# Cross attention and mixture of experts on one core: products twelve blocks behind the scores, splits and sums placed anew

## The reference

```python
def xattn(q, k, v, gamma):           # q = layernorm(x); k = v = ctx
    qk = einsum('bhdq,bhdl->bhql', qh, kh) / sqrt(dq)
    sm = softmax(qk, axis=-1)
    ret = einsum('bhql,bhdl->bhdq', sm, vh)
    return gamma * ret
x = x + xattn(layernorm(x), ctx, ctx, gamma)
def ffn(x, U, V, W1, b1, W2, b2):
    h = relu(x @ W1 + b1)
    alpha = softmax(h @ W2 + b2)     # 8 experts
    vx = einsum('krd,bsd->bskr', V, x)
    return einsum('bsk,bskd->bsd', alpha, einsum('kdr,bskr->bskd', U, vx))
x = x + ffn(layernorm(x), ...)
```

## Time and profile before

| | |
|---|---|
| three runs | 1687.66 us median (1683.01 to 1691.62) |
| the profiled execution | 1685.4 us, its span 1683.6 us |
| TensorE | 1568.5 us busy, 93% |
| VectorE | 993.7 us, 59% |
| ScalarE | 765.0 us, 45% |
| GpSimd | 715.3 us, 42% |
| DMA queue 1 | 56.3% of 16 engines' span, 293.84 MB |

### The profile page before, as it was taken

One profiled execution on the slowest core, in us unless ns is written; L12 is line 12 of the kernel. 1 busy time (PEld: TensorE's weight loads), 2 busy tenths in 40 slices (PEclk: granted clock), 3 DMA queues, 4 the chain that ended last, 5 costly groups with the idle time before them and its releaser, 6 DMA issues.

```text
span 1683.6 us, 21711 instructions
## 1 busy us (share of the span) xinstructions
PE 1568.5 (93%) x6496; PEld 1159.5 (69%) x6496; DVE 993.7 (59%) x1290; ACT 765.0 (45%) x1222; POOL 715.3 (42%) x523
## 2 busy tenths in 40 slices
PE   5989999898999989999967999999999999999999
PEld 3666666666666666666645787877878787787877
DVE  7888888888888888888754432433323242332312
ACT  5776766767676676767653312112121211212120
POOL 3887878888788887878751000000000000000000
PEclk9999999999999999999987999999999999999999
DMA  6989989999899888998886031120302112030302
GB/s 176 283 270 287 264 285 273 275 286 267 285 262 290 281 268 284 264 294 277 240 265 220 20 101 50 63 87 6 130 13 100 50 62 87 10 133 6 100 1 75
DMA packets 119963, 294.18 MB, mean 175 GB/s; under 512 B 26240, under 2 KB 31360, under 8 KB 119936
## 3 DMA queue, kind: packets, MB, share of 16 engines
q1 hardware_dynamic: 119936, 293.84, 56.3%
HBM read 125.87 MB, written 33.69 MB: 95 GB/s over the span
## 4 chain that ended last, share of the span: by engine, by line
PE 49%; POOL 26%; issue 15%; DMA 4%; SPq 3%; DVE 2%; ACT 1%; POOLq 0%; ACTq 0%; DVEq 0%
PE scores L928 21%; POOL pt_lo L342 15%; PE scores L971 11%; PE attended L989 10%; POOL k_lo L325 4%; POOL x_out L351 3%; PE spare L1008 2%; DMA x_res<-in_x 2%; SPq L223 2%; POOL v_lo L329 2%; PE scores L517 1%; PE scores L946 1%; PE scores L943 1%; DMA pt<-pb 1%; PE attended L539 1%
## 5 line engine op out<-in xcount | busy, mean ns | idle before, releaser
L342 POOL TENSOR_TENSOR pt_lo<-pt,pt_hi 128x512 fp32r<-128x512 f32 (+1 forms) x256 | 399.7, 1562 | 156.5 <-ACT pt_hi L411 156.5
L571 DVE TENSOR_REDUCE neg_max<-scores 128x1 f32<-128x1024 f32 x256 | 312.6, 1221 | 105.8 <-PE scores L517 105.5
L418 ACT ACTIVATE probs<-scores,neg_max 128x1024 f32<-128x1024 f32 x256 | 284.2, 1110 | 198.8 <-DVE neg_max L571 198.5
L580 DVE STREAM_TRANSPOSE pb<-probs 128x1024 f32<-128x1024 f32 x256 | 316.2, 1235 | 16.8 <-DMA pt<-pb 16.5
L853 POOL TENSOR_TENSOR rstd<-var_eps,minus_half 128x1 f32<-128x1 f32 x28 | 17.2, 613 | 609.6 <-DVE var_eps L1054 609.6
L517 PE MATMUL scores<-k_hi,q_hi 128*128 128x512 f32 x512 | 237.1, 544 | 20.5 <-ACT probs L418 11.3
L539 PE MATMUL attended<-pt_hi,v_hi 128*128 128x512 f32 x320 | 140.9, 440 | 88.4 <-POOL pt_lo L342 87.6
L411 ACT ACTIVATE pt_hi<-pt 128x512 fp32r<-128x512 f32 (+1 forms) x256 | 186.7, 729 | 63.8 <-DMA pt<-pb 59.2
L872 ACT ACTIVATE hidden<-scores,b_col 128x512 f32<-128x512 f32 x64 | 44.2, 690 | 351.3 <-PE scores L928 351.3
L928 PE MATMUL scores<-nt_hi,w_hi 128*128 128x512 f32 x512 | 200.9, 392 | 2.5 <-DVE w_lo L1079 2.5
L928 PE MATMUL scores<-nt_lo,w_hi 128*128 128x512 f32 x512 | 200.2, 391 | 0.0
(11 more groups left out here) (95 smaller groups left out, 2640.9 us busy)
## 6 DMA issues: line engine op xcount, KB each, us to landing
pt<-pb SPq DMA_DIRECT2D x512, 256.0 KB, 4.6
x_raw<-in_x SPq DMA_DIRECT2D x32, 512.0 KB, 6.3
k_raw<-in_ctx SPq DMA_DIRECT2D x32, 512.0 KB, 5.2
gain_row<-gains SPq DMA_DIRECT2D x64, 256.0 KB, 4.8
x_res<-in_x SPq DMA_DIRECT2D x32, 512.0 KB, 5.6
x<-x_out SPq DMA_DIRECT2D x64, 256.0 KB, 4.1
first_n<-x SPq DMA_DIRECT2D x32, 512.0 KB, 3.6
result<-x SPq DMA_DIRECT2D x64, 256.0 KB, 3.7
```

The lines of the kernel that those rows point to most:

```text
L342: nc.gpsimd.tensor_tensor(pt_lo[2 * parity + half][:, :, keys, :], pt[2 * parity + half][:, :, keys, :], as_f32(hi[half][q][:]), ALU.subtr ...
L418: nc.scalar.activation(probs[j % 2][:], scores[j % 2][:], ACT.Exp, bias=neg_max[:, j:j + 1], accum_out=row_sum[b][:, j:j + 1]).then_inc(s_ ...
L571: nc.vector.tensor_reduce(neg_max[:, j:j + 1], scores[j % 2][:], AX_X, ALU.max, negate=True).then_inc(s_max, 1)
L580: nc.vector.transpose(pb[half][:, :, j % HALF, :], probs[j % 2][:]).then_inc(s_blocks, 1)
```

## The change

The distance from scores to products becomes 12 blocks, for the low parts 10, for the high parts 9. The pieces of work beside them move to other blocks of the head. SP's queue gets another order: `load_v` fetches the values of the head that runs (before: of the next one) and stands behind the gather of the previous head's second half; each `spread_gain` stands a few issues behind its own `send_gain` and ahead of the next gather. Heads 1 to 3 are written out.

```diff
-    LAG = 10
+    LAG = 12
+    LOW_LAG = 10
+    HIGH_LAG = 9
@@ over_heads
-        slot(1, JB, 1, False, False)
-        with eng.Fori(1, heads // 2 - 1) as pair:
+        for h in range(1, 4):
+            slot(h, h * JB, h % 2, False, False)
+        with eng.Fori(2, heads // 2 - 1) as pair:
@@ sync, slot
             if not first:
                 gather(h - 1, n - JB, 1, 1 - parity)
+                sp.wait_ge(s_vlo, h)
+                load_v(h)
                 send_gain(h - 1, 0)
...
                 load_k(h + 2)
+            if not first:
+                spread_gain(h - 1, 0)
             if not (known and h < 2):
                 sp.wait_ge(s_pv, n - JB)
             load_v_native(h, parity)
-            if not last:
-                sp.wait_ge(s_vlo, h + 1)
-                load_v(h + 1)
-            if not first:
-                spread_gain(h - 1, 0)
+            if more:
+                sp.wait_ge(s_q32, h + 2)
+                load_x(h + 2)
+            gather(h, n, 0, parity)
             if not first:
                 send_gain(h - 1, 1)
...
                 load_residual(h - 1)
-            if more:
-                sp.wait_ge(s_q32, h + 2)
-                load_x(h + 2)
-            gather(h, n, 0, parity)
-            if not first:
                 spread_gain(h - 1, 1)
@@ gpsimd, slot
-                low_probs(quarter_in(h, n, j, parity, LAG - 1))
-                if j == 1 and not last:
+                low_probs(quarter_in(h, n, j, parity, LOW_LAG))
+                if j == 1 and not early:
+                    add_residual(h - 2, 0)
+                if j == 2 and not last:
                     low_keys(h + 1, 1 - parity)
-                if j == 3:
+                if j == 3 and not last:
+                    scale_of_queries(h + 1, 1 - parity)
+                if j == 5 and not early:
+                    add_residual(h - 2, 1)
+                if j == 6 and not last:
+                    low_queries(h + 1, 1 - parity)
+                if j == 7:
                     low_values(h, parity)
...
@@ scalar, slot
-                if j == 0 and not first:
+                if j == 1 and not first:
                     gains(h - 1, 0)
-                if j == 4 and not first:
+                if j == 5 and not first:
                     gains(h - 1, 1)
-                high_probs(quarter_in(h, n, j, parity, LAG - 2))
-                if j == 0 and not last:
+                high_probs(quarter_in(h, n, j, parity, HIGH_LAG))
+                if j == 1 and not last:
                     high_keys(h + 1, n + JB, 1 - parity)
-                if j == 2:
+                if j == 4:
                     high_values(h, n, parity)
-                if j == 3 and not last:
+                if j == 4 and not last:
                     queries(h + 1, 1 - parity)
@@ vector, slot
+                if j in (0, 4) and not early:
+                    scale_attended(h - 2, n - 2 * JB, j // 4)
+                if j in (0, 4) and not first:
+                    inverse_sums(h - 1, j // 4, 1 - parity)
+                if j in (1, 2) and not last:
+                    statistics(h + 1, 1 - parity, j - 1)
+                if j == 3 and not last:
                     variance(h + 1, 1 - parity)
...
```

More of the change, by code:

```diff
@@ L364, in slot @@
             for j in range(JB):
-                low_probs(quarter_in(h, n, j, parity, LAG - 1))
-                if j == 1 and not last:
+                low_probs(quarter_in(h, n, j, parity, LOW_LAG))
+                if j == 1 and not early:
+                    add_residual(h - 2, 0)
+                if j == 2 and not last:
                     low_keys(h + 1, 1 - parity)
-                if j == 3:
-                    low_values(h, parity)
[L370 to L377, removed]
+                if j == 3 and not last:
[5 more added lines that the diff above has]
+                if j == 7:
+                    low_values(h, parity)
                 if last and j in (4, 6):
@@ L390, in gpsimd @@
         for j in range(JB):
-            low_probs(quarter_in(h, n, j, 0, LAG - 1))
+            low_probs(quarter_in(h, n, j, 0, LOW_LAG))
+            if j == 1:
+                add_residual(h - 2, 0)
             if j in (1, 2):
                 first_factor(j + 1)
-            if j == 3:
+            if j == 5:
                 add_residual(h - 2, 1)
-            if j == 7:
-                add_residual(h - 1, 0)
-        low_probs(quarter_in(h + 1, n + JB, 0, 1, LAG - 1))
+        for j in range(2):
+            low_probs(quarter_in(h + 1, n + JB, j, 1, LOW_LAG))
+        add_residual(h - 1, 0)
         add_residual(h - 1, 1)
@@ L490, in scalar @@
         for j in range(4):
-            high_probs(quarter_in(h, n, j, 0, LAG - 2))
+            high_probs(quarter_in(h, n, j, 0, HIGH_LAG))
             first_high(j)
-        gains(h - 1, 1)
         normalise_first(2)
         normalise_first(3)
+        gains(h - 1, 1)
         for j in range(4, JB):
-            high_probs(quarter_in(h, n, j, 0, LAG - 2))
+            high_probs(quarter_in(h, n, j, 0, HIGH_LAG))
             first_high(j)
+        high_probs(quarter_in(h + 1, n + JB, 0, 1, HIGH_LAG))
     def tensor(pe):
@@ L564, in tensor @@
             turn_first(j)
-        for j in range(2):
+        for j in range(4):
             attended_products(quarter_in(h + 1, n + JB, j, 1, LAG))
@@ L635, in slot @@
                 maxima(n + j, j)
-                if j == 2 and not last:
+                if j == 3 and not last:
                     dve.wait_ge(s_stat, h * 2 + 4)
@@ L641, in slot @@
                     blocks(n + j - 1, j - 1, h)
-                if j < 2 and not last:
-                    statistics(h + 1, 1 - parity, j)
-                if j == 2 and not last:
-                    variance(h + 1, 1 - parity)
[L646 to L653, removed]
+                if j in (0, 4) and not early:
[4 more added lines that the diff above has]
+                    statistics(h + 1, 1 - parity, j - 1)
+                if j == 3 and not last:
+                    variance(h + 1, 1 - parity)
                 if last and j in (3, 5):
@@ L664, in vector @@
         blocks(n - 1, JB - 1, h - 1)
+        scale_attended(h - 2, n - 2 * JB, 0)
+        inverse_sums(h - 1, 0, 1)
         first_statistics(2)
         first_statistics(3)
-        low_first(0)
-        low_first(1)
+        dve.wait_ge(s_vlo, h)
+        for u in range(4):
+            low_first(u)
         scale_attended(h - 2, n - 2 * JB, 1)
         inverse_sums(h - 1, 1, 1)
[L671 to L674, removed]
+        for u in range(4, 2 * FIRST):
+            low_first(u)
         scale_attended(h - 1, n - JB, 0)
-        low_first(6)
-        low_first(7)
         scale_attended(h - 1, n - JB, 1)
```

## The result

The changed kernel takes 1732.2 us (median of 4 runs, 1731.8 to 1733.3) against 1686.0 (1683.0 to 1691.6): 1.028 times as long, 95% interval 1.026 to 1.030. The forecast was 1719 in a range of 1675 to 1750, with 0.73 for slower.

What follows compares the result with a forecast made beforehand. SP's in-order queue was taken to set the head period, rising from 26.54 to 27.5 us: 29 × 0.96 = 27.8, + 6.7 + 2.3 − 3.7 = 33.1 us on 1685.4, forecast 1719 us, range 1675 to 1750.

Steps and rivals of the forecast that it cites:

- B: SP's queue from the gather of half 1 to the next of half 0: forecast 15.0 us per head.
- A: SP's queue from the gather of half 0 to that of half 1, including a send's landing: 12.5 us per head.
- over the gains: From gather 1 to gather 0 on SP, waiting for the other send's landing before its spread: 14.3 us.
- over v: From gather 1 to gather 0 through v's landing, ScalarE's split, the query and x_raw's issue: 14.95 us.
- ScalarE waits some 4 us for v_raw: Expected sign in the profile after: ScalarE reaches v's split before v lands, some 4 us per head.
- the gains alone bind: Rival: v lands early enough and only the sends' waits set SP's period, 26.8 us per head, 1698 us; chance 0.13.
- The ends: Start, last head and drain of the attention, outside the 29 head periods: +6.7, +2.3 and −3.7 us.
- +6.7: Start: later queries of head 1 and v_raw's way delay its gather of half 1 from 58.95 to 65.6 us.
- +2.3: Last head: first_n's load 0.8 us later in the queue, plus the longer stretch between the last two gathers.
- −3.7: Drain: low parts precede the last adds, so the last scaling waits only for gain_row, at 892.8 instead of 896.46.
- the skipped chain of waits: Engine waits behind the gathers, TensorE's for low parts 60.1 us in 700, which greater distances would remove, promising a gain.
- The faster rival: Rival: quick sends (1.4) and v (3.9) leave SP's queue short; another loop binds at 24.3 us per head, 1626 us; chance 0.15.

Runs made afterwards that it cites:

- the fastest kernel: Changed kernel with sends on ScalarE's queue, v loaded half a head earlier, x_raw behind the gather of half 0, q_lo at block 5: 1593.8 us, ratio 0.947.

## Why the prediction was right

*The place.* The head period is set by SP's queue, and the distances can't shorten it. Right: 50 waits where 8 were, the single spread moved ahead of a gather in the kernel before costs 45 us by itself, and taking both waits away from the changed one gives 66 back.

*The terms.* The period was put at 27.5 us and is 28.07. B came out at 15.04 for 15.0; the missing time is in A, 13.04 for 12.5. The mis-sized term is the landing of a send behind a gather: 4.3 was taken from 26 single ones, and the 50 of the changed kernel have a median of 4.6, v's own 4.7 for 4.9:

```profile
DMA to landing us min/median/max: 3.5/4.6/6.0
DMA to landing us min/median/max: 3.9/4.7/6.2
```

In A the landing is 0.3 of what is missing, and the issues and gaps around it are the rest. In B the sum had two ways, over the gains at 14.3 and over v at 14.95. The way over the gains was put too short by 0.7, for the landing (0.3), v_raw's issue with its gap (1.1 instead of 0.85 us) and gaps; v's was put 0.2 too long. So they are nearly equal: SP waits for the query in 13 of 25 heads only and 0.3 us per head. That B fits to 0.1 is in part luck, since the way that was said to end last ends last in half of the heads. "ScalarE waits some 4 us for v_raw" came out at 2.7: it comes to the split some 9.6 us behind the gather's start (7.6 + 4.7 − 2.7) and not 8.5. One reading was off without weight: the spread that landed after 4.3 us is the second of the 26; the first, at 110.91, took 5.2.

*The rest of the way.* v mattered as a way of its own, which the rival "the gains alone bind" denied: with the sends' waits gone B stays at 15.2 us, and only with v early as well is it 13.6. By its sum v should have been worth 0.65 us per head, 19 us. Its removal gives 29, since v's issue also leaves B.

*The ends.* +6.7 was +5.7; +2.3 was +4.4; −3.7 was −6.4. Together +3.7 where 5.3 was said. Of the +4.4 nothing comes from first_n, which was put at 0.8: VectorE waits 10.3 us for it instead of 5.5, but the last gather of half 0 starts 21.0 us behind the gather before it, as in the kernel before (21.1). All of it is A between the last two gathers, 13.7 us for 9.2. In the drain the last spread was issued 27.6 us behind the last gather's start (29.1 before), and the scaling began 3.4 behind it where a landing of 4.7 was said.

*The rivals.* The gain that the skipped chain of waits promised was real: 27 us for distances and places with the queue in order, held back by SP. The faster rival's condition, sends landing in 1.4, did not come true, 3.5 was the least. With the waits removed by hand (1636, 25.1 us per head) the kernel lies near the 1626 and 24.3 worked out for it. That says little for the loop in that sum, since TensorE then waited for q_lo, which is not in it, and with q_lo earlier and x_raw behind the gather the time went to 1594.

## What to carry to other kernels

An engine that issues DMAs in order is a resource like the others: add up one period of its queue, issues and waits, stretch by stretch between the transfers that others wait for, before crediting a gain to any wait elsewhere. Slack in one stretch doesn't cover a wait in another. A transfer whose completion is needed by the same queue belongs on another queue or many issues earlier, and its reader has a latest place too, so read both ends. A greater distance in a pipeline pays only once what feeds it runs at the pace of the engines.

## What the runs showed of the hardware

The granted clock of TensorE fell in the changed kernel, from 1.00 to 0.94 of full speed as a mean over 100 to 800 us. Windows of 4 us show where: after a hole of 2.79 us that ends at 304.55 and one of 2.97 us that ends at 332.45.

```profile
304.00:308.00 4.00, 3.45 (x9) 2.72 (x10) 2.10 (x2) 2.83 (x7) 2.71 (x2) 0.63 0.82 295
308.00:312.00 4.00, 4.00 (x16) 2.90 (x16) 2.94 (x4) 1.88 (x4) 4.00 (x4) 0.95 0.97 329
332.00:336.00 4.00, 3.55 (x9) 2.83 (x10) 1.83 (x2) 2.72 (x7) 2.82 (x2) 0.57 0.93 290
```

The busy share of the DMA engines was no fixed price of the transfers. In the changed kernel it is 0.89 at 28.1 us per head, which is 25.0 us of busy time and was taken as a floor when the runs were planned; in the fastest kernel it is 0.95 at 23.6 us, which is 22.4, for the same transfers. So a high share alone doesn't say that DMA binds.

A send of 2 KB took 4.2 us in the median from ScalarE's queue too (4.6 from SP's in the changed kernel), with gathers under way in SP's. Whether it lands faster with no other traffic was not tried.
